# A fused attention and expert block: halves of keys and queries taken from PSUM, projections in another order, and the last block's two sequences routed one by one

## The reference

```python
x = x + tanh(g_xattn[0]) * attention(layernorm(x), ctx, ctx, wq, bq, wk, bk, wv, bv, wo, bo)
xn = layernorm(x) * gamma + beta
logits = clip(xn @ Wr.T, -1e4, 1e4)
probs = softmax(logits); top_p, top_i = top_k(probs, 2)
rank = place of each (token, choice) among those of the same expert, in order of tokens
kept = rank < 640
buf[expert, rank] = xn                       # the rest is dropped
y = (silu(buf @ Wg.T) * (buf @ Wu.T)) @ W3.T # per expert, 256 -> 1024 -> 256
x = x + tanh(g_ffn[0]) * sum over the 2 choices of y * top_p * kept
```

## Time and profile before

| what | us |
|---|---|
| three runs of the kernel | 535.59, 535.72, 539.57 (median 535.72) |
| the profiled execution, its own time | 534.19 |
| its span in the trace | 532.3 |
| start to the first scores | 19.05 |
| eight attention blocks and the tail up to the first expert product | 19.05 to 236.68 |
| experts | 236.68 to 532.3 |

### The profile page before, as it was taken

How to read it: one execution, slowest core, us unless ns; L and a number is a source line. 1 busy time by engine, 2 the same in 40 slices (tenths; PEclk the granted TensorE clock), 3 DMA queues, 4 the chain that set the end, 5 groups by cost and what they waited for, 6 DMA issues and landing times.

```text
span 532.3 us, 10749 instructions
## 1 busy us (share of the span) xinstructions
PE 479.7 (90%) x3551; PEld 444.7 (84%) x3551; DVE 360.8 (68%) x854; ACT 298.9 (56%) x757; POOL 208.9 (39%) x272
## 2 busy tenths in 40 slices
PE   5699999899999877369998999999999999999991
PEld 4588887777877666269998999999999999999991
DVE  6867888988888997547876574485843768544240
ACT  3689878677778764416664564373723747423230
POOL 8636776787787566510212012203032030311202
PEclk9999999999999997779999999999999999999996
DMA  8868432314142611153677362347451474201111
GB/s 269 209 140 250 78 41 72 75 57 81 42 80 55 205 42 53 58 175 118 234 184 219 78 226 34 60 129 193 132 144 20 130 188 131 31 4 17 13 19 20
DMA packets 41649, 57.33 MB, mean 108 GB/s; under 512 B 3721, under 2 KB 38576, under 8 KB 39552
## 3 DMA queue, kind: packets, MB, share of 16 engines
q1 hardware_dynamic: 35168, 48.62, 31.7%
q0 software_dynamic: 6144, 8.07, 9.1%
q10 hardware_dynamic: 288, 0.00, 0.0%
HBM read 36.24 MB, written 16.72 MB: 99 GB/s over the span
## 4 chain that ended last, share of the span: by engine, by line
PE 55%; DVE 3%; issue 2%; POOL 1%; DMA 0%; ACT 0%; POOLq 0%; DVEq 0%
PE bank L1438 17%; PE bank L1440 17%; PE bank L1439 17%; PE bank L1432 2%; PE bank L1361 1%; PE bank L1304 1%; POOL expert_rows L484 0%; DMA expert_rows<-xr,slotu 0%; DVE pT L929 0%; PE bank L1290 0%; POOL out_tokens L546 0%; DVE nm L924 0%; PE bank L1231 0%; PE bank L1238 0%; DVE osum L938 0%
## 5 line engine op out<-in xcount | busy, mean ns | idle before, releaser
L546 POOL DMA_INDIRECT out_tokens<-ysc,rows x32 | 49.6, 1550 | 245.6 <-DVE ysc L1142 238.9
L1438 PE MATMUL bank<-bXh,wh 128*128 128x384 f32 (+1 forms) x384 | 122.1, 318 | 2.9 <-issue 2.6
L1440 PE MATMUL bank<-bXh,wl 128*128 128x384 f32 (+1 forms) x384 | 121.8, 317 | 0.0
L1439 PE MATMUL bank<-bXl,wh 128*128 128x384 f32 (+1 forms) x384 | 121.8, 317 | 0.0
L749 ACT ACTIVATE sil<-bank 128x384 f32<-128x384 f32 (+1 forms) x96 | 43.7, 456 | 128.4 <-PE bank L1440 127.2
L1121 DVE TENSOR_TENSOR hF<-sil,bank 128x384 f32<-128x384 f32 (+1 forms) x96 | 48.9, 510 | 77.9 <-ACT sil L749 71.3
L633 ACT ACTIVATE p<-bank,nm 128x128 f32<-128x128 f32 x256 | 73.6, 387 | 14.7 <-DVE nm L924 14.7
L1438 PEld LDWEIGHTS bank<-bXh,wh 128*128 128x128 f32 x384 | 72.7, 189 | 3.3 <-issue 3.3
L1438 PE MATMUL bank<-wh,hH 128*128 128x256 f32 x256 | 73.8, 288 | 0.3 <-DVE ysc L1142 0.3
L1439 PEld LDWEIGHTS bank<-bXl,wh 128*128 128x128 f32 x384 | 72.7, 189 | 0.0
L1440 PEld LDWEIGHTS bank<-bXh,wl 128*128 128x128 f32 x384 | 72.6, 189 | 0.0
(11 more groups left out here) (146 smaller groups left out, 878.8 us busy)
## 6 DMA issues: line engine op xcount, KB each, us to landing
stage<-in_w12T SPq DMA_DIRECT2D x16, 1024.0 KB
stage<-in_w3T SPq DMA_DIRECT2D x8, 1024.0 KB
expert_rows<-padrow SPq DMA_DIRECT2D x8, 662.5 KB, 7.9
rows<-expert_rows SPq DMA_DIRECT2D x7, 662.5 KB, 4.4
kM<-k SPq DMA_DIRECT2D x64, 64.0 KB, 2.4
cT<-in_ctxT SPq DMA_DIRECT2D x8, 256.0 KB, 3.1
out_tokens<-x_all SPq DMA_DIRECT2D x8, 256.0 KB, 2.3
x_all<-in_x SPq DMA_DIRECT2D x2, 640.0 KB, 8.5
```

The lines of the kernel that those rows point to most:

```text
L546: pool.indirect_dma_start(out=out, out_offset=bass.IndirectOffsetOnAxis(rows[par][:, c, D + E:ROW].bitcast(U32), 0), in_=ysc[par][:, c, :] ...
L1438: nc.tensor.matmul(out_ap, ah, bh, start=start, stop=False)
L1439: nc.tensor.matmul(out_ap, ah, bl, start=False, stop=False)
L1440: return nc.tensor.matmul(out_ap, al, bh, start=False, stop=stop)
```

## The change

ACT writes the high halves straight from PSUM, and the scale of the queries goes into the inputs' columns:

```diff
-                act.activation(xT[:, :, :], Xp[:, :].rearrange("p (c t) -> p c t", c=DC), ACT.Copy).then_inc(act_xT, 1)
+                act.activation(xT[:, :, :], Xp[:, :].rearrange("p (c t) -> p c t", c=DC), ACT.Copy, scale=HD ** -0.5).then_inc(act_xT, 1)
...
-                    act.activation(qT[:, t, :], bank[:, t * SB * T:(t + 1) * SB * T], ACT.Identity,
-                                   bias=bq4[:, t:t + 1], scale=HD ** -0.5).then_inc(act_q32, 1)
-                act.wait_ge(act_q32, DC * (n + 1))
-                act.activation(q2[par][:, 0, :, :], qT[:, :, :], ACT.Copy).then_inc(act_q, 1)
+                    act.activation(q2[par][:, 0, t, :], bank[:, t * SB * T:(t + 1) * SB * T], ACT.Identity, bias=bq4[:, t:t + 1])\
+                       .then_inc(act_qh, 1)
...
-                    act.activation(kT[:, t, :], bank[:, t * SB * T:(t + 1) * SB * T], ACT.Identity, bias=bqkv[:, 1, t:t + 1])\
-                       .then_inc(act_k32, 1)
...
-                act.activation(k2[:, 0, :, :], kT[:, :, :], ACT.Copy).then_inc(act_kT, 1)
+                    act.activation(k2[:, 0, t, :], bank[:, t * SB * T:(t + 1) * SB * T], ACT.Identity, bias=bqkv[:, 1, t:t + 1])\
+                       .then_inc(act_kh, 1)
```

The low halves move from POOL to DVE, keys in group 2 and queries in group 5 (both behind the group's maxima), and the reciprocals of the heads' sums go to PSUM, behind the heads' outputs in their banks:

```diff
-                pool.tensor_tensor(k2[:, 1, :, :], kT[:, :, :], k2[:, 0, :, :].bitcast(F32), ALU.subtract).then_inc(pool_kl, 1)
...
-                pool.tensor_tensor(q2[par][:, 1, :, :], qT[:, :, :], q2[par][:, 0, :, :].bitcast(F32), ALU.subtract).then_inc(pool_ql, 1)
...
+            def keys_low(n, bank):
+                dve.wait_ge(act_kh, DC * (n + 1))
+                for t in range(DC):
+                    ins = dve.scalar_tensor_tensor(k2[:, 1, t, :], bank[:, t * SB * T:(t + 1) * SB * T], bqkv[:, 1, t:t + 1],
+                                                   k2[:, 0, t, :].bitcast(F32), ALU.add, ALU.subtract)
+                ins.then_inc(dve_kl, 1)
...
-        orec = sb(pa, "orec", [P, 8], F32)
...
+        orec = [O[i][:, 8 * VW:8 * VW + 8] for i in range(2)]
```

PE makes values in group 0, keys in 1, the inputs' transposes in 3 and queries in 4, and the ranks behind the last products of group 7:

```diff
-                        if g == 2:
+                        if g == 0:
+                            values(n + 1, 1 - par, Xp)
+                        elif g == 1:
                             keys(n + 1, 1 - par, Xp, use)
-                        elif g == 4:
-                            queries(n + 1, Xp)
-                        elif g == 6:
-                            pe.wait_ge(act_q32, DC * (n + 2))
-                            values(n + 1, 1 - par, Xp)
+                        elif g == 3:
+                            input_columns(n + 1, False, not prev1)
```

The ranks have no running count; the members of every sequence are kept and added up anew, from a base that holds the expert's first slot:

```diff
-                nc.tensor.matmul(rk, onesb[:, :], seen[:, :].unsqueeze(1).to_broadcast([P, SB, E]), start=False, stop=True)\
-                    .then_inc(pe_rk, 1)
...
+                nc.tensor.matmul(rk, onesb[:, :], ebase[:, :].unsqueeze(1).to_broadcast([P, w, E]), start=True, stop=False)
+                for j in range(first):
+                    nc.tensor.matmul(rk, onesb[:, :], member[:, j, :].unsqueeze(1).to_broadcast([P, w, E]), start=False, stop=False)
+                pe.wait_ge(dve_mem, s + 1)
```

POOL splits a block's values in the block before (values_rest and values_third of n + 1 ahead of the second norm2), and sends the last rows in another order:

```diff
-                    values_third(n, par)
...
+                    values_rest(n + 1, 1 - par)
+                    values_third(n + 1, 1 - par)
...
+            rows_known(NSB - 2, None)
+            scatter(0, 0, 0)
             norm2(NSB - 1, 1)
+            scatter(0, 0, 1)
+            for j in range(SB):
+                scatter(0, 1, j)
...
-            dispatch(NSB - 2, 0)
-            dispatch(NSB - 1, 1)
+            dispatch(NSB - 1, 1, 0)
+            dispatch(NSB - 1, 1, 1)
```

PE, ACT and DVE route the last block's two sequences one after the other, on PE so:

```diff
+            for one, bk in ((0, S[0]), (1, S[1])):
+                pe.wait_ge(act_exp, G - 1 + one)
+                x2_columns(NSB - 1, 1, bk, one)
+                logits(NSB - 1, bk, one)
+                if one == 0:
+                    keep_running(O[0], 8)
+                pe.wait_ge(dve_lg, NSB + one)
+                ranks(NSB - 1, bk, one)
```

422 lines of the change are left out of this document (220 added, 202 removed).

## The result

The changed kernel took 541.35 us (median of 20 runs, 539.07 to 546.98), the kernel before 535.54 beside it (20 runs). The ratio of the two is 1.011, with a 95% interval of 1.0081 to 1.0139: slower by 1.1%, where 520 us had been forecast. The profiled execution took 546.98 us, the slowest of the 20; its span is 545.1 us, 12.8 above that of before. Two rows of its page, busy time and granted clock, stand against the earlier trace rows.

The account below looks back on a forecast made before the run. It took TensorE, with VectorE nearly as full, to bound blocks 3 to 6, and VectorE block 7. Terms -1.6, -0.4, -6.9, -3.0 and -3.9 sum to -15.8: 534.19 to 518.4, 520 as median; range 510 to 530.

Parts of the forecast that it names:

- The scaling product: Scaling the heads' outputs on VectorE: one input in PSUM ends its wait for GpSimd, 839 to 291 ns, 28 times.
- VectorE's load: VectorE's busy time in blocks 4 and 6 falls by 1.0 us to about 20.3 us.
- The wait for GpSimd's values goes: TensorE's 6.2 us of waits for the last third of the values go, as it is made a block earlier.
- Blocks 3 to 6 at 22.6: Each block takes TensorE's busy 22.3 us plus 0.3 of new waits; 90.4 against 97.32 us, -6.9.
- the second rival: Waits in the blocks pass from GpSimd to VectorE's low halves in groups 5 to 7; -4 us, 532; chance 0.11.
- Blocks 1 and 2 at 0 and -0.4: Block 1 has no idle TensorE, so 0; block 2 lasts 22.38 us with 21.97 busy, so -0.4.
- Start and block 0 at -1.6: Up to block 0's end, TensorE's wait for the spread keys shortens by 1.6 us; bounds +1 and -3.
- Block 7 at -3.0: Block 7 falls from 19.57 us to VectorE's 15.6 plus about 1 of latency; bounds 0 and -3.9.
- The tail at -3.9: The last scatter starts at 223.9 instead of 227.77 us, with the last slots 0.9 us later; bounds -4.7 and -1.8.
- The experts carried over at 295.6: The experts' stage, 295.62 us with TensorE busy 281.48, is untouched by the change and stays as it was.
- They went round once or twice, so hardly a list is longer: Writing out the middle blocks' loops costs no instruction fetching, since hardly any engine's instruction list grows.
- The third rival: Slower: VectorE becomes the bound of blocks 3 to 6, 25.9 for 24.33 us each; 543 us; chance 0.07.

Follow-up runs that it names:

- lock_back: The changed kernel with the reciprocals of the row sums in SBUF again; 543.68 us, 1.0149 of the kernel before.
- order_back: The changed kernel with the order of products, copies and GpSimd's value parts of before, all else kept; 540.68 us, 1.0093 of the kernel before.
- vf_first: The changed kernel with ScalarE's copy of the values ahead of group 0's exponentials; 538.80 us, 1.0048 of the kernel before.
- slots_late: The changed kernel with VectorE's slot instructions moved behind the next block's largest scores of group 0; 536.68 us, 1.0031 of the kernel before.
- lock_alone: The kernel before with only the reciprocals of the row sums put in PSUM; 533.48 us, 0.9952 of the kernel before.
- first_values: The changed kernel with GpSimd's parts of block 0's values ahead of its wait for the bias sum; 538.38 us, 1.0033 of the kernel before.
- warm_tail: The changed kernel with extra transposes keeping TensorE at work in the tail; 539.64 us, 1.007 of the kernel before.
- before_longer: The kernel before with 70 tiny products that nobody reads behind the counts; 540.61 us, 1.0109 of the kernel before.

## Why the forecast was wrong

The forecast of 520 us was 21.3 below the median. By the profiled execution (518.4 forecast, 546.98 measured, 28.6 apart) the parts of it are: start and block 0 3.9 us, blocks 1 and 2 3.4, blocks 3 to 6 7.8, block 7 1.5, the tail 3.2, the experts 8.8. Two steps failed. The new order of the products was given no cost, and it took back what the attention blocks were to gain; and the experts were carried over unchanged.

**The scaling product** was forecast at 291 ns and measured at 288; against 839 ns, 28 of them come to 15.4 us of VectorE less. Right in size. But lock_back shows that the rest of the change had taken most of the excess away (median 294 ns with the reciprocals in SBUF), so the reading "GpSimd holds it" was right and the credit to PSUM too large. The rule of the Trainium skill (SBUF — State Buffer, Who interferes with whom) agrees with both traces: 288 ns with one input in SBUF, and with two up to 525, or 294 where GpSimd is not in the way. But the trouble did not go away with oN. Small instructions are held too, L917 by 0.54 us in each of blocks 3 to 7. One such, the guard in order_back, has a single input in SBUF, which the rule as the prediction gives it would leave alone. The dearer source in PSUM that the Trainium skill has (VectorE: DVE Perf Modes, The TRN2 errata) does not show: 286 to 290 ns against 291 at least.

**VectorE's load**: 20.3 us forecast for blocks 4 and 6, 19.5 measured. Right, and better.

**The wait for GpSimd's values goes**: right, and for the reason given, the place of the values; order_back has it back with 7.1 us.

**Blocks 3 to 6 at 22.6**: wrong, 24.56. The step that failed is "The order of the four products changes and their number does not": the order had no term. I asked what stands behind the new low halves on VectorE, and not what stands ahead of the values' copy on ScalarE. I named the first rest of the values as late next; what was late is the copy of the values themselves, and with it the keys, as both share one bank. It costs 1.0 us per block (vf_first, slots_late). Most of another 1.1 is waits for the low halves of the probabilities, 6.7 us from 59 to 199 us. For them I had written "they cost nothing while TensorE has its long products in groups 0, 1 and 4 to work off; ... I take 0.3", and 0.3 per block is what the halves on VectorE cost in the old order (order_back against lock_alone, 1.8 us); the other 3.8 us came with the new order. That is the second rival in kind, and by the sign that I gave for it (above 24): the waits change hands. Its place was not the one I had given it, groups 5 to 7, alone, but the block's boundary too.

**Blocks 1 and 2 at 0 and -0.4**: wrong, +1.8 and +1.2. I took a block without idle TensorE as one that cannot lose. order_back gives back all of block 2 and half of block 1, so the order did it; the rest of block 1 is open.

**Start and block 0 at -1.6**: the start gained 1.3, near the 1.6 forecast; block 0 lost 3.55, past my bound of +1. I had looked at "VectorE's other early work" and not at GpSimd's: the copy of block 1's values used to come in group 6, long after the parts of block 0's; now it comes in group 0, where those are still to be made (first_values).

**Block 7 at -3.0**: -1.5. VectorE's busy 15.6 was right (15.96); the latency around it was put at 1 us and is 2.1 (18.05 less 15.96).

**The tail at -3.9**: -0.7. The two sequences' slots and the scatters behind them:

```profile
224.74 0.17 DVE L923 TENSOR_REDUCE slotu<-pslot 128x2 uint32<-128x16 f32 x1
...
225.80 0.98 POOL L472 DMA_INDIRECT expert_rows<-xr,slotu  x1 [1.56 <-DVE slotu L923]
...
228.40 0.16 DVE L923 TENSOR_REDUCE slotu<-pslot 128x2 uint32<-128x16 f32 x1
...
231.03 0.97 POOL L472 DMA_INDIRECT expert_rows<-xr,slotu  x1 [0.30 <-DVE past L1102]
```

The last slots stand 25.3 us behind the eighth scores, against 22.9, so the term "I take 0.9 us" was 2.4. From the last slots to the start of the last scatter I had 1.5 us, and it took 2.5. So the last scatter starts 27.9 us behind the eighth scores against 29.3, a gain of 1.4 and not of 3.9. Half of this went behind it: the mean clock was 0.64 and not 0.73, and the 22 empty transposes and the six of the rows behind the last scatter took 4.93 and 1.15 us, against 4.45 and 0.82. warm_tail won 4 us back in its execution. I had no term for the clock.

**The experts carried over at 295.6**: wrong, 304.4 in the profiled execution, where it is the largest single term (8.8), and 300.5 to 303.3 in variants with the same number of products to within two. In these, blocks 3 to 6 are the larger one (7.8). "They went round once or twice, so hardly a list is longer" was about the loops and true of them; but the ranks, the base and the counts make TensorE's list 73 products longer, 20 of which the prediction itself had counted in blocks 3 to 6, and before_longer shows that 70 products more by themselves make a kernel 1.1% slower. The third rival has nearly the right time, 543, for a wrong reason: VectorE did not become longer.

## What to carry to other kernels

An order that frees an engine is worth what the next handover leaves of it. Before moving a product to the start of a block, follow the one bank it writes through each engine that must empty it, with what stands ahead of that copy, in the steady block and in the first one, where the buffers' earlier readers run late.

An instruction of VectorE that GpSimd holds is seen by its longest against its median. When it has been cured, look for the next one that is held: it was a routing instruction of 0.2 us here, and which one it was changed with the order.

Compare stages at the same events, also those that the change does not touch. If an untouched stage moves, look for idle times that have no semaphore behind them, and try the same number of empty instructions in the old kernel before blaming the change.

## What was not expected of the hardware

TensorE's stops of 2.4 to 5.1 us in a stretch that no edit touches depend on how many products stand before it; 70 to 73 more make them two, 131 more one again, and each holds one transfer of 16384 bytes of instructions. The granted clock was at its half level (0.50 from 273.30 to 276.20) right behind the first stop of the changed kernel, which had left TensorE idle for 5.1 us; but such a stop does not always bring it down: behind 2.61 us it stayed full in the kernel before, and behind 2.59 us in lock_alone it fell. An instruction of VectorE on 16 columns took 0.74 us in place of 0.21 where it began 0.02 us behind one of GpSimd's. The scaling product with an input in PSUM was no slower than with both in SBUF, 286 to 290 ns against 291.
